# Latent attention's rotary exchange on VectorE, and a reordered end of the image-text projections

## The reference

```python
# L1_attn: latent attention, ROPE = 64, causal mask
q = (x @ wq).reshape(b, s, 16, 128 + 64); q_nope, q_pe = q[..., :128], q[..., 128:]
c, k_pe = (x @ wkv_a)[..., :128], (x @ wkv_a)[..., 128:]
# rotate: re = xe*cos - xo*sin ; ro = xo*cos + xe*sin   (xe, xo: even and odd features)
q_pe, k_pe = _apply_rope(q_pe, cos, sin), _apply_rope(k_pe, cos, sin)
k_nope, v = split((c @ wkv_b).reshape(b, s, 16, 128 + 128))
attn = softmax(causal((q_nope . k_nope + q_pe . k_pe) / sqrt(192))); out = (attn @ v) @ wo
x = layernorm(x + out)
# L1_xattn: image keys are context[:, :257], text keys context[:, 257:], head size 32
q     = rms_norm(x @ q_w + q_b) * norm_q_w
k_img = rms_norm(ctx_img @ k_img_w + k_img_b) * norm_k_img_w
k     = rms_norm(ctx_txt @ k_w + k_b) * norm_k_w
out   = (softmax(q k^T / sqrt(32)) @ v + softmax(q k_img^T / sqrt(32)) @ v_img) @ o_w + o_b
```

## Time and profile before

| | |
|---|---|
| median of 3 executions | 2328.51 us (2325.72 to 2328.53) |
| the profiled execution | 2316.98 us, span 2315.2 us |
| busy: PE, DVE, ACT, POOL | 94%, 62%, 51%, 20% of the span |
| granted TensorE clock, mean | 0.978 of full speed |
| four quads' units and attention | 1398.7 to 1780 us |
| image-text projections | 1780 to 1919 us |
| image-text attention | 1919 to about 2120 us |

### The profile page before, as it was taken

How to read it: one execution, slowest core, us unless ns; L and a number is a source line. 1 busy time by engine, 2 the same in 40 slices (tenths; PEclk the granted TensorE clock), 3 DMA queues, 4 the chain that set the end, 5 groups by cost and what they waited for, 6 DMA issues and landing times. The chain is left out here.

```text
span 2315.2 us, 35594 instructions
## 1 busy us (share of the span) xinstructions
PE 2182.3 (94%) x13410; PEld 1720.5 (74%) x13410; DVE 1444.6 (62%) x3965; ACT 1172.8 (51%) x3016; POOL 465.4 (20%) x383
## 2 busy tenths in 40 slices
PE   9998999999999999999977988999899998997998
PEld 5645788888888888888866965665655884665987
DVE  2385777787778777777657435454555456883535
ACT  2153767676767676766543424453443445771222
POOL 1210212221222212221111002223232000220533
PEclk9999999999999999999998999999999998998999
DMA  6013111100111111100003023213212310003100
GB/s 243 7 64 112 37 35 38 38 16 30 37 38 38 36 36 38 37 10 26 10 1 146 1 76 123 100 64 127 80 76 99 137 52 20 2 2 147 71 1 29
DMA packets 44772, 131.94 MB, mean 57 GB/s; under 512 B 6535, under 2 KB 21671, under 8 KB 40119
## 3 DMA queue, kind: packets, MB, share of 16 engines
q1 hardware_dynamic: 32792, 108.59, 12.8%
q0 software_dynamic: 2304, 12.58, 1.3%
q10 hardware_dynamic: 9504, 8.50, 1.2%
HBM read 109.10 MB, written 20.15 MB: 56 GB/s over the span
## 5 line engine op out<-in xcount | busy, mean ns | idle before, releaser
L782 PE MATMUL psum<-qa_kv_raw,context 128*128 128x256 f32 (+1 forms) x1536 | 343.6, 380 | 0.0
L782 PEld LDWEIGHTS psum<-qa_kv_raw,context 128*128 128x128 f32 (+1 forms) x1536 | 277.2, 184 | 44.9
L768 PE MATMUL psum<-qa_w,qa_xq 128*100 128x256 bf16 (+1 forms) x3072 | 267.0, 247 | 3.1 <-PEq L60 3.1
L768 PEld LDWEIGHTS psum<-qa_w,qa_xq 128*100 128x100 bf16 x3072 | 256.1, 126 | 4.1 <-issue 4.0
L884 ACT ACTIVATE qa_prob<-psum,qa_nm 100x361 f32<-100x361 f32 x128 | 72.0, 562 | 168.3 <-DVE qa_nm L1016 168.3
L2473 ACT ACTIVATE it_prob<-psum,it_nm 100x257 f32<-100x257 f32 (+1 forms) x256 | 101.9, 412 | 42.0 <-DVE it_nm L2497 41.8
L839 PE MATMUL psum<-qa_catq,qa_o 128*128 128x400 f32 x512 | 111.9, 361 | 9.9 <-DVE X L1055 6.0
L1108 POOL TENSOR_TENSOR qa_w<-qa_w_raw,qa_w 128x768 bf16<-128x768 f32 x28 | 46.0, 1643 | 371.0 <-DVE qa_w L958 371.0
L978 DVE BATCH_NORM_STATS2 qa_st<-psum 100x6 f32<-100x128 f32 x320 | 69.7, 284 | 78.7 <-PE psum L768 78.7
L1114 POOL TENSOR_TENSOR qa_o<-qa_o_raw,qa_o 128x512 fp32r<-128x512 f32 x32 | 40.6, 1270 | 350.5 <-DVE qa_o L966 350.5
L1007 DVE TENSOR_SCALAR qa_nrm_t<-psum,qa_mv,qa_sd 100x128 f32<-100x128 f32 x320 | 107.9, 404 | 2.4
(11 more groups left out here) (355 smaller groups left out, 5013.6 us busy)
## 6 DMA issues: line engine op xcount, KB each, us to landing
qa_w_raw<-in_qa_w SPq DMA_DIRECT2D x8, 1536.0 KB, 6.7
la_gf_raw<-in_gf_w SPq DMA_DIRECT2D x16, 768.0 KB, 4.4
gf_w<-gf_ternary SPq DMA_DIRECT2D x4, 3072.0 KB, 25.4
qa_piece<-in_tf_pieces ACTq DMA_DIRECT2D x64, 128.0 KB, 2.1
qa_o_raw<-in_qa_o SPq DMA_DIRECT2D x8, 1024.0 KB, 5.1
gf_ternary<-la_gf_made POOLq DMA_DIRECT2D x8, 768.0 KB, 3.6
gf_ternary<-gf_last_made POOLq DMA_DIRECT2D x8, 768.0 KB, 3.6
context<-in_context SPq DMA_DIRECT2D x8, 722.0 KB, 12.4
```

The costliest lines, as they stand in the source:

```text
L768: mm = pe.matmul(psum[0:T, 2 + at // 512, at % 512:at % 512 + width], xq[:, kind, k, b * T:(b + 1) * T], w3[:, s, part, k, at:at + width], ...
L782: mm = pe.matmul(psum[0:rows, i // 2, (i % 2) * 256:(i % 2) * 256 + 256], ctxT[:, k, b * TC + t0:b * TC + t0 + rows], kv_raw[:, s, k, :], ...
```

## The change

**Exchange by VectorE.** `w_a` loses its third block, PE's "swap" units and `neg_swap` are gone. A new helper `turn` on DVE makes `by_cos` in one instruction and `by_sin` in four instructions of 32 partitions each: each reads PSUM and the sine table at the partner rows (start partition r0 xor 32) and writes at r0. `k_rot` and `q_rot` are then `by_cos` minus `by_sin`, both in SBUF. A quad has 12 units, and the tables that place the ternary weights' steps are rewritten for 12; DVE takes a scale out in the same place of its order as PE sums it.

**Projections.** Ten groups: keys 0, 1, first half of the queries, keys 2, 3, the whole second half of the queries, keys 4 to 7. A group's sum over partitions and its root stand between chunk 1 and chunk 2 of the next group. After the last group PE computes the scores of the first two pairs there, before the last group's sum over partitions. The last group (keys of batch 7) is not scaled in this stage.

**Attention.** DVE takes the last group's reciprocal at batch 1, pair 0, and scales its four chunks at pairs 1 to 4, two instructions each (`normalise_last`); PE waits for it before batch 7. The first scores and DVE's waits for them are gone, and the semaphore counts shifted by two. The result `oT` goes into the buffer Y.

```diff
@@ -1674,18 +1674,17 @@
-    prepare = {0: 0, 4: 1, 10: 2}
-    sum_after = {2: (0, 0), 4: (0, 1), 6: (0, 2), 8: (1, 0), 10: (1, 1), 12: (1, 2), 14: (2, 0)}
+    prepare = {0: 0, 4: 1, 8: 2}
+    sum_after = {2: (0, 0), 4: (0, 1), 5: (0, 2), 6: (1, 0), 8: (1, 1), 10: (1, 2), 11: (2, 0)}
     sum_beside = {1: (2, 1), 4: (2, 2)}
-    scale_after = {q + 1: xy for q, xy in sum_after.items()}
-    make_after = {7: 0, 13: 1}
+    make_after = {5: 0, 10: 1}
     X, psum = core.X, core.psum
...
         for i in range(4):
-            units += [("q", i, half), ("rot" if i < 2 else "swap", i % 2, half)]
-    takes_out = {"q": "act", "rot": "dve", "swap": "dve"}
+            units += [("q", i, half)] + ([("rot", i, half)] if i < 2 else [])
+    takes_out = {"q": "act", "rot": "dve"}
     RING = 6
@@ -1817,7 +1812,7 @@
-            for i in range(3):
+            for i in range(2):
@@ -1831,8 +1826,7 @@
-            pe.wait_ge(S_["lat_out"], 6)
-            pe.wait_ge(S_["swap_ready"], 5)
+            pe.wait_ge(S_["krot_parts"], 8)
@@ -1841,15 +1835,11 @@
                         e, count = taken(q - RING)
-                        pe.wait_ge(S_[e], g * per_quad[e] + count)
+                        pe.wait_ge(S_[e], (g * per_quad[e] + count) * (4 if e == "dve" else 1))
                     bank = q % RING
-                    if kind in ("q", "rot"):
-                        for k in range(C):
-                            mm = pe.matmul(psum[:, bank, 0:HALF], (w_q if kind == "q" else w_rot)[:, k, i * P:(i + 1) * P],
-                                           X[:, k, cols(h)], start=(k == 0), stop=(k == C - 1))
-                    else:
-                        pe.wait_ge(S_["dve"], unit_out(g, ("rot", i, h)))
-                        mm = pe.matmul(psum[:, bank, 0:HALF], neg_swap[:, :], by_sin[:, i, :], start=True, stop=True)
+                    for k in range(C):
+                        mm = pe.matmul(psum[:, bank, 0:HALF], (w_q if kind == "q" else w_rot)[:, k, i * P:(i + 1) * P],
+                                       X[:, k, cols(h)], start=(k == 0), stop=(k == C - 1))
                     mm.then_inc(S_["unit_mm"], 1)
@@ -1857,7 +1847,7 @@
-                pe.wait_ge(S_["dve"], g * per_quad["dve"] + per_quad["dve"])
+                pe.wait_ge(S_["qrot_ready"], g * per_quad["dve"] + per_quad["dve"])
@@ -2009,27 +1999,29 @@
+            def turn(raw, i, done):
+                dve.tensor_tensor(by_batch(by_cos[:, i, :]), by_batch(raw), four(cos), ALU.mult).then_inc(S_["turned"], 1)
+                for r0 in range(0, P, ROPE // 2):
+                    to, at = slice(r0, r0 + ROPE // 2), slice(r0 ^ ROPE // 2, (r0 ^ ROPE // 2) + ROPE // 2)
+                    last = dve.tensor_tensor(by_batch(by_sin[to, i, :]), by_batch(raw[at]),
+                                             sin[at, :].unsqueeze(1).broadcast_to([ROPE // 2, 4, T]), ALU.mult)
+                    last.then_inc(done, 1)
...
-                dve.wait_ge(S_["lat_mm"], 6)
+                dve.wait_ge(S_["lat_mm"], 4)
...
-                dve.tensor_tensor(by_batch(by_cos[:, h, :]), by_batch(psum[:, 2 + h, 0:HALF]), four(cos), ALU.mult).then_inc(S_["lat_out"], 1)
-                dve.tensor_tensor(by_batch(by_sin[:, h, :]), by_batch(psum[:, 4 + h, 0:HALF]), four(sin), ALU.mult).then_inc(S_["lat_out"], 1)
+                turn(psum[:, 2 + h, 0:HALF], h, S_["krot_parts"])
...
-            dve.wait_ge(S_["lat_out"], 6)
+            dve.wait_ge(S_["turned"], 2)
+            dve.wait_ge(S_["krot_parts"], 8)
...
-                                      ALU.add).then_inc(S_["krot_ready"], 1)
+                                      ALU.subtract).then_inc(S_["krot_ready"], 1)
...
-            dve.memset(neg_swap[:, :], 0.0).then_inc(S_["swap_ready"], 1)
-            dve.wait_ge(S_["swap_ready"], 1)
-            for r0 in range(0, P, ROPE // 2):
-                c0 = r0 ^ (ROPE // 2)
-                dve.tensor_scalar(neg_swap[r0:r0 + ROPE // 2, c0:c0 + ROPE // 2],
-                                  core.ident[r0:r0 + ROPE // 2, r0:r0 + ROPE // 2], -1.0, None, ALU.mult).then_inc(
-                    S_["swap_ready"], 1)
@@ -2041,22 +2033,18 @@
-                    if takes_out[kind] != "dve":
-                        continue
-                    dve.wait_ge(S_["unit_mm"], g * len(units) + q + 2)
...
-                        if h:
-                            dve.wait_ge(S_["dve"], unit_out(g, ("swap", i, 0)))
-                        dve.tensor_tensor(by_batch(by_cos[:, i, :]), by_batch(psum[:, q % RING, 0:HALF]), four(cos),
-                                          ALU.mult)
-                        dve.tensor_tensor(by_batch(by_sin[:, i, :]), by_batch(psum[:, q % RING, 0:HALF]), four(sin),
-                                          ALU.mult).then_inc(S_["dve"], 1)
-                    elif kind == "swap":
-                        dve.wait_ge(S_["dve"], unit_out(g, ("rot", i, h)))
-                        dve.tensor_tensor(q_rot[:, i, cols(h)], by_cos[:, i, :], psum[:, q % RING, 0:HALF],
-                                          ALU.add).then_inc(S_["dve"], 1)
-                    if q in scale_after:
-                        x, y = scale_after[q]
+                        n = g * per_quad["dve"] + taken(q)[1] - 1
+                        dve.wait_ge(S_["unit_mm"], g * len(units) + q + 2)
+                        if n >= 2:
+                            dve.wait_ge(S_["qrot_ready"], n - 1)
+                        turn(psum[:, q % RING, 0:HALF], i, S_["dve"])
+                        dve.wait_ge(S_["turned"], n + 3)
+                        dve.wait_ge(S_["dve"], 4 * n + 4)
+                        dve.tensor_tensor(q_rot[:, i, cols(h)], by_cos[:, i, :], by_sin[:, i, :],
+                                          ALU.subtract).then_inc(S_["qrot_ready"], 1)
+                    if q in sum_after:
+                        x, y = sum_after[q]
@@ -2126,28 +2114,38 @@
-        image_text_projections(nc, core, a, Y, qn, kT, v, values, last, scratch, stored)
+        rms = outer.enter_context(nc.sbuf_tensor("itp_rms", [P, 2, HALF], F32))
+        image_text_projections(nc, core, a, Y, qn, kT, v, rms, values, last, scratch, stored)
...
-        oT = outer.enter_context(nc.sbuf_tensor("it_oT", [P, C, N], F32))
-        image_text_attention(nc, core, a, qn, kT, v, last_rows, oT)
+        image_text_attention(nc, core, a, qn, kT, v, rms[:, 1, 0:TC], last_rows, Y)
...
-def image_text_projections(nc, core, a, Y, qn, kT, v, values, last, scratch, stored):
+def pair_scores(pe, psum, qn, kT, b, p):
+    for j in range(2):
+        h = 2 * p + j
+        rows = slice((h % 4) * HD, (h % 4 + 1) * HD)
+        mm = pe.matmul(psum[0:T, 2 * (p % 2) + j, 0:TC], qn[rows, h // 4, b * T:(b + 1) * T],
+                       kT[rows, h // 4, b, :], start=True, stop=True)
+    return mm
+def image_text_projections(nc, core, a, Y, qn, kT, v, rms, values, last, scratch, stored):
...
-    groups = [("k", 0, 0, TC), ("k", 1, 0, TC), ("q", 0, 0, HALF)] + [("k", b, 0, TC) for b in range(2, B)] + [
-        ("q", 1, 0, QUARTER), ("q", 1, QUARTER, HALF)]
+    groups = [("k", 0, 0, TC), ("k", 1, 0, TC), ("q", 0, 0, HALF), ("k", 2, 0, TC), ("k", 3, 0, TC), ("q", 1, 0, HALF)] + [
+        ("k", b, 0, TC) for b in range(4, B)]
...
-        sq, rms, std = sb("sq", [P, C, HALF]), sb("rms", [P, 2, HALF]), sb("std", [P, N])
+        sq, std = sb("sq", [P, C, HALF]), sb("std", [P, N])
@@ -2233,6 +2231,8 @@
                     q = n * C + c
+                    if n and c == 2:
+                        square_sum(n - 1)
                     if q >= 4:
@@ -2244,8 +2244,10 @@
                     mm.then_inc(S_["kq_mm"], 1)
-                if n:
-                    square_sum(n - 1)
+            pe.wait_ge(S_["kq_out"], len(groups) * C)
+            pe.wait_ge(S_["normed"], groups.index(("q", 0, 0, HALF)) + 1)
+            for p in range(2):
+                pair_scores(pe, psum, qn, kT, 0, p)
             square_sum(len(groups) - 1)
@@ -2267,6 +2269,8 @@
                 for c in range(C):
+                    if n and c == 2:
+                        root(n - 1)
                     act.wait_ge(S_["kq_mm"], n * C + c + 1)
@@ -2276,8 +2280,6 @@
                 act.activation(sq[:, :, 0:width(g)], place(g), ACT.Square).then_inc(S_["sq_ready"], 1)
-                if n:
-                    root(n - 1)
             root(len(groups) - 1)
@@ -2313,6 +2315,8 @@
                     dve.tensor_tensor(into, into, other, ALU.add).then_inc(S_["sq_summed"], 1)
+                if n + 1 == len(groups):
+                    continue
                 dve.wait_ge(S_["rms_ready"], n + 1)
@@ -2375,11 +2379,9 @@
-                for j in range(2):
-                    h = 2 * p + j
-                    rows = slice((h % 4) * HD, (h % 4 + 1) * HD)
-                    mm = pe.matmul(psum[0:T, 2 * (p % 2) + j, 0:TC], qn[rows, h // 4, b * T:(b + 1) * T],
-                                   kT[rows, h // 4, b, :], start=True, stop=True)
```

(23 more changed lines are left out.)

18 lines of the change are left out of this document (7 added, 11 removed).

## The result

The change makes the kernel slower: 2407.2 us (median of 4 executions, 2405.0 to 2407.4) against 2327.1 for the kernel before beside it (2321.1 to 2328.5). The ratio is 1.0364, its 95% interval 1.0323 to 1.0406: some 80 us lost where 16 were forecast as gain.

The account below looks back on a forecast made before the run. It took DVE and POOL to limit the latent attention, PE the attention with DVE close behind. Gains 2.9 + 3.4 + 5.95 + 7.7 less 3.6 made 16.4 us: 2328.5 to 2312.1, range 2300 to 2320.

Parts of the forecast that it names:

- Keys scaled in the attention: Attention, batch 1: moving the last keys' reciprocal and scalings to DVE there costs 3.6 us (2.5 to 6).
- Reciprocal, 1.4 us reach PE: Attention, batch 1: the 2.42 us reciprocal meets 0.78 idle, is 1.6 late; 1.4 reach PE through transposed probabilities.
- Chunks 0.3 each: Attention, next four steps: chunks of 0.66 us meet idle gaps near 0.5 but cost about 0.3 each.
- 1 us more at POOL: Attention: the fourth chunk meets POOL's 1.88 and 1.03 us instructions, costing 1 us more.
- Queries' half, 5.95: Projections: the queries' second half in one group takes 10.75 us instead of 16.7, a gain of 5.95.
- Tail, 7.7 (6.5 to 8.9): Projections' end (U, last matmuls' end): step loop begins at U + 12.8 against U + 20.5, gain 7.7 us.
- about a third busy: Projections' tail: PE's load in the 6 us before the attention, the reason for putting `keep_busy` at 6.5 us.
- The two together: Projections and their tail: gains of 5.95 us for the queries' half and 7.7 us for the tail.
- Start of latent attention, 2.9: Latent attention's start: units begin at 1395.8 instead of 1398.7, a gain of 2.9 us (1 to 4).
- Quads, 0.85 each: Latent attention's quads: `la_nm` free at 43.6 instead of 44.4 us, gain 0.85 a quad, 3.4 for four.
- the second: Small-gain rival: quads gain nothing, start 1.5, `keep_busy` at low clock 6.6, scaling costs 5; 2319.5 us, chance 0.2.
- The one for slower: Latent units: dearer 32-partition instructions make DVE the bound, deciding from 1.1 us each; 2351 us at 1.42; chance 0.04.

Follow-up runs that it names:

- waits filled: Changed kernel with 5 and 9 unread matmuls of 128 x 112 where TensorE waits in batch 1: 2304.4 us, ratio 0.9954.
- everything covered: Changed kernel with the last keys' reciprocal and all four pairs of scalings moved under the keep-busy matmuls: 2299.3 us, ratio 0.9944.
- the latent part alone: Kernel before with only the change's latent attention, projections and image-text attention as before: 2313.2 us, ratio 0.9992.
- the wait filled: Changed kernel with all keys' scaling under keep-busy, plus five unread 128 x 400 matmuls in each latent quad's wait: 2293.7 us, ratio 0.9902.
- the reciprocal moved: Changed kernel with only the reciprocal moved under the keep-busy matmuls, scalings left in batch 1: 2398.1 us, ratio 1.0345.
- the locked scaling: Kernel before plus one key-chunk scaling on unread data at batch 1, fifth pair, beside GpSimd's 1.88 us multiply: 2409.1 us, ratio 1.0438.
- the refill: Changed kernel plus eight keep-busy matmuls (128 x 400) before the first weighing of batch 2: 2320.0 us, ratio 1.001.

## Why the prediction was wrong

The step that failed is *Keys scaled in the attention*, and in it the unspoken assumption that a microsecond in which PE waits costs a microsecond. The term was put at 3.6 us. At a held clock it is about that; in the changed kernel it cost some 93 (80 lost plus the 13 gained ahead; in the two profiles the step loop is 103 longer), because the granted clock fell from 1.00 to 0.50 at the first wait and stayed there for 54 pairs.

- *Reciprocal, 1.4 us reach PE.* It is 1.1: the step with the wait takes 3.70 us, and the same step in the kernel before 2.57.
- *Chunks 0.3 each.* Nothing in the steps that transpose reciprocal sums (2.56 or 2.57 us with a chunk and without one), 0.1 in a step without (2.48 against 2.39).
- *1 us more at POOL.* It is 1.9 (a step of 4.27 against 2.39): the lock was foreseen, its length not. A scaling that begins 0.65 behind GpSimd's start ends 1.28 behind its end.
- With the clock held (waits filled) all of this costs 3.5 us in the step loop (168.30 us to the output projection, against 164.81 with everything covered), close to the 3.6. The whole times are 5.1 apart (2304.4 and 2299.3), but they are of two chips. What was missing from the sum is what the wait does to the clock of the 54 pairs that follow.
- *Queries' half, 5.95.* It is 5.1: from the first projection matmul to U the kernel before takes 116.45 us and the changed one 111.31. The 16.7 us that two pieces were said to take hold a sum over partitions (0.7 us from 1899.91 on), which the changed kernel still pays.
- *Tail, 7.7 (6.5 to 8.9).* It is 5.9, below its bounds: the loop begins at U + 14.65, against 20.52. The attention starts at U + 6.1 as forecast, but `keep_busy` at 8.61 was 0.9 dearer than the upper bound of 7.7. PE had stood still ahead of it, in the few us that were called "about a third busy", and the clock was at 0.68 from 1903 to 1911.
- *The two together.* In whole times the version with the keys under cover lies 13.9 below the one with the latent part alone (2299.3 and 2313.2, same call), close to the 13.65 forecast. That agreement is in part luck: of the 16.2 us between their profiles these two terms make 11.1, and nearly all the rest lies ahead of the latent attention (2.2) and behind the step loop (2.5), where the two are alike.
- *Start of latent attention, 2.9.* The first unit starts 2.7 sooner behind the first `w_a` matmul (24.24 against 26.91), close to the forecast, with instructions of `by_sin` 0.60 apart. But PE waits 4.35 us in one piece instead of 1.45 and runs the first unit at half clock: 1.5 given back.
- *Quads, 0.85 each.* `la_nm` is free 43.4 behind the first unit against 44.4, a gain of 1.0, as forecast. Most of it is eaten by the fall of the clock behind the 4 us wait: from the first quad's first scores to the fourth's it takes 282.4 us, before 283.5, so 0.4 a quad. With the wait filled it takes 277.8.
- *Rivals.* None of them named the clock of the step loop; the second named a low clock, but of `keep_busy` alone. The one for slower (the exchange makes VectorE the bound) had another mechanism; its condition, instructions of 1.1 us, did not come about.

The waits and locks that the prediction named came about, most at nearly the forecast size, and the sign was wrong all the same, because all terms were sums of busy and idle time at a fixed clock. The rows had two warnings. The prediction counted the freed PE time of a quad as "PE then stands waiting for `la_nm`", at no cost. And the granted clock of 0.70 at `keep_busy` showed that waits cost clock; `keep_busy` itself stands in this kernel for no other purpose, and I costed it as a delay, at half or full clock, without asking what the loop behind it needed.

The Trainium skill, *TensorE: Matmul & The Clock Gate*, section "Loop structure matters more than you think", says "Whether your matmuls stay warm is determined by your loop nest", and counts VectorE's copies out of PSUM among the things that don't break it. The traces agree with the first. The second is said of a loop in which the next matmuls follow at once, and here they didn't: PE waited for just such copies (`it_pT`), 0.92 and 1.81 us long, and the clock fell at both.

## What to carry to other kernels

A loop of small matmuls, as this one, may hold TensorE's full clock and be unable to regain it; there a wait isn't priced by its length but by all that runs behind it. Before moving work onto the engine that such a loop waits for, look at the granted clock in the stretches ahead and behind, put the work under a stretch where TensorE has dense matmuls of its own, and keep VectorE instructions with two SBUF inputs away from GpSimd's. Where the wait can't be avoided, a few matmuls on an unused PSUM bank that nobody reads were a cheap insurance here (3.5 us in the loop, VectorE's own delays included, where some 93 had been lost); and when PE work is removed, ask what TensorE will do in the time that comes free.

## What the runs showed of the hardware

- A wait of 1.8 us in the step loop took the clock to 0.50 in all nine executions that had it alone (five with the reciprocal moved, four of the kernel before with the locked scaling; one of each by its stretches, the others by their time and a mean clock of 0.931 to 0.935). A wait of 0.91 in the kernel before did it in five of ten. In the changed kernel a wait of 0.92 did it in all 14 executions seen (four of it, ten with the refill behind it; again one of each by its stretches). Why the same 0.9 us is always too much there and half the time in the kernel before stays open. PE's steps up to the wait are alike in the two profiles (2.39, 2.64, then 3.70 us with it), the fall comes within 2.5 us behind its end, and the scalings that follow had lengthened no step by then.
- Once at 0.50, some 230 us of the loop's matmuls with 8.00 of 8 us busy didn't bring it back; 6.9 us of 128 x 400 matmuls did, and so did the output projection's behind the loop (0.62 from 2183 to 2191, 1.00 from 2191 on).
- The kernel before may be near the edge itself: its two long executions lost 110 and 135 us, at a mean clock of 0.924 and 0.918. No stretches of them are on record, so that it is the same fall is an inference from the size and the mean clock.
- Its spread of 17 us without them is larger than that of any version with the change (2 to 3 us within a call). The latent attention took 401.4, 408.3 and 410.0 us in three profiles of the same code. In the two long ones three or more of the 10 us stretches from 1600 on are at a granted clock under 0.9, in the short one only one; what tips them was not looked into. Such a difference, up to 8.6 us in a stage that no edit touched, is as large as several terms of the sum.
